# Transposed mixings of a four-layer graph network, done graph by graph on 64 rows of TensorE

## The reference

```python
h = relu(layernorm(x))
# layer 0: hypergraph convolutions: with H = (adj != 0), a node is mixed as D^-1 H B^-1 H^T (h @ W)
# layer 1: three graph convolutions
support = einsum('bnf,fh->bnh', h, W)
h = einsum('bnm,bmh->bnh', adj, support) + b
# layer 2: three diffusion steps with a learned transition matrix
# layer 3: mean of the neighbours, concatenated with x, times W
x = x + out
```

## Time and profile before

| | |
|---|---|
| median of 3 runs | 2702.6 us (2702.22 to 2703.21) |
| profiled execution, its own time | 2700.35 us |
| its span, first to last instruction | 2698.5 us |
| granted clock of TensorE | 0.999 of full |
| PE / PEld busy | 2655.7 us (98%) / 2218.4 us (82%) |
| DVE / ACT / POOL busy | 1924.8 (71%) / 1216.2 (45%) / 1153.9 us (43%) |

### The profile page before, as it was taken

One profiled execution on the slowest core, in us unless ns is written; L12 is line 12 of the kernel. 1 busy time (PEld: TensorE's weight loads), 2 busy tenths in 40 slices (PEclk: granted clock), 3 DMA queues, 4 the chain that ended last, 5 costly groups with the idle time before them and its releaser, 6 DMA issues.

```text
span 2698.5 us, 44877 instructions
## 1 busy us (share of the span) xinstructions
PE 2655.7 (98%) x13218; PEld 2218.4 (82%) x13218; DVE 1924.8 (71%) x4504; ACT 1216.2 (45%) x2231; POOL 1153.9 (43%) x2022
## 2 busy tenths in 40 slices
PE   7999999999999999999999998999999999999999
PEld 4888888888888888888888887888888888888887
DVE  7777777777777665656665668777777777777776
ACT  4444444434444554545454553322222222566665
POOL 5444444444444733333333346212112122677776
PEclk9999999999999999999999999999999999999999
DMA  4111111111111312111111122111111111344443
GB/s 136 39 40 47 38 38 36 45 45 35 41 33 44 109 34 66 37 62 43 56 45 54 49 82 88 57 54 54 56 52 48 54 54 64 114 148 152 134 139 124
DMA packets 136299, 178.58 MB, mean 66 GB/s; under 512 B 54464, under 2 KB 54464, under 8 KB 136256
## 3 DMA queue, kind: packets, MB, share of 16 engines
q1 hardware_dynamic: 131072, 168.62, 19.4%
q10 hardware_dynamic: 5184, 9.44, 1.2%
HBM read 110.90 MB, written 67.11 MB: 66 GB/s over the span
## 4 chain that ended last, share of the span: by engine, by line
PE 93%; DVE 2%; issue 1%; ACT 1%; POOL 1%; DMA 0%; SPq 0%; ACTq 0%; POOLq 0%; DVEq 0%
PE ps L464 27%; PE ps L466 27%; PE ps L465 26%; PE ps L481 6%; PE ps L506 4%; PE ps L484 2%; POOL w_lo L1272 1%; ACT row_hi L698 0%; DVE row_lo L948 0%; ACT w_hi L698 0%; PE ps L584 0%; PE ps L580 0%; ACT normed L738 0%; DVE adj_both L948 0%; POOL vecs L1297 0%
## 5 line engine op out<-in xcount | busy, mean ns | idle before, releaser
L464 PE MATMUL ps<-w_hi,col_hi 128*128 128x512 f32 x2752 | 1099.4, 399 | 2.6 <-POOL w_lo L1272 1.1
L466 PE MATMUL ps<-w_hi,col_lo 128*128 128x512 f32 x2752 | 1075.3, 391 | 0.0
L465 PE MATMUL ps<-w_lo,col_hi 128*128 128x512 f32 x2752 | 1072.5, 390 | 0.0
L466 PEld LDWEIGHTS ps<-w_hi,col_lo 128*128 128x128 f32 x2752 | 516.8, 188 | 112.5
L464 PEld LDWEIGHTS ps<-w_hi,col_hi 128*128 128x128 f32 x2752 | 517.4, 188 | 107.1 <-issue 5.1
L465 PEld LDWEIGHTS ps<-w_lo,col_hi 128*128 128x128 f32 x2752 | 518.4, 188 | 97.9 <-issue 0.2
L1305 POOL TENSOR_TENSOR var_eps<-moments,eps_ln 128x1 f32<-128x1 f32 x256 | 55.2, 216 | 924.4 <-DVE moments L965 924.4
L698 ACT ACTIVATE col_hi<-ps 128x512 fp32r<-128x512 f32 x448 | 255.5, 578 | 257.3 <-PE ps L484 133.8
L952 DVE TENSOR_TENSOR wide<-ps,col_hi 128x512 f32<-128x512 f32 x256 | 175.5, 686 | 146.9 <-ACT col_hi L698 145.5
L698 ACT ACTIVATE row_hi<-ps 128x512 fp32r<-128x512 f32 x224 | 132.9, 593 | 304.3 <-PE ps L466 302.9
L1272 POOL TENSOR_TENSOR row_lo<-normed,row_hi 128x512 fp32r<-128x512 f32 x128 | 165.1, 1301 | 214.0 <-ACT row_hi L698 213.9
(11 more groups left out here) (155 smaller groups left out, 4169.3 us busy)
## 6 DMA issues: line engine op xcount, KB each, us to landing
out<-x_res SPq DMA_DIRECT2D x256, 256.0 KB, 2.0
x_in<-out SPq DMA_DIRECT2D x192, 256.0 KB, 2.8
x_in<-x SPq DMA_DIRECT2D x64, 256.0 KB, 2.6
x_res<-out SPq DMA_DIRECT2D x64, 256.0 KB, 3.1
adj_in<-adj_t SPq DMA_DIRECT2D x96, 64.0 KB, 2.4
raw<-w ACTq DMA_DIRECT2D x12, 256.0 KB, 2.7
raw<-wk ACTq DMA_DIRECT2D x12, 256.0 KB, 2.7
raw<-w_t ACTq DMA_DIRECT2D x10, 256.0 KB, 3.0
```

The costliest lines, as they stand in the source:

```text
L464: nc.tensor.matmul(out_ap, lhs_hi, rhs_hi, start=start, stop=False, **checks)
L465: nc.tensor.matmul(out_ap, lhs_hi, rhs_lo, start=False, stop=False, **checks)
L466: return nc.tensor.matmul(out_ap, lhs_lo, rhs_hi, start=False, stop=stop, **checks)
```

## The change

The two graphs of a tile are mixed apart. For feature block `k` and graph `h`, the stationary operand is the 64 rows of that graph in `row_hi`, the moving one the graph's own 64x64 block of both halves of the adjacency (2x64 = 128 columns); with `row_lo` it is 64 columns. The result of graph 0 goes to bank 0 of the slot and that of graph 1 to bank 1. In the program, each such matmul stands in a tile of the array of 64 rows by 128 columns, at row 0 or at row 64; all others use 128 by 128. The readers of the result take the new layout (`graphs`, `halves`), and the semaphore counts twice, once for each graph.

```diff
         def halves(t):
-            both = ps[:, t, :, :].rearrange("p a (k h n) -> p (a k) h n", h=2, n=P)
-            return both[:, :, 0, :], both[:, :, 1, :]
+            both = ps[:, t, :, :].rearrange("p g (k h n) -> p g k h n", h=2, n=N)
+            return both[:, :, :, 0, :], both[:, :, :, 1, :]
+
+        def graphs(ap):
+            return ap.rearrange("p (k g n) -> p g k n", g=2, n=N)
...
-            def mix_transposed(t):
+            def mix_transposed(t, done):
                 for k in range(KB):
-                    at = ps[:, t, k // 2, (k % 2) * 2 * P:(k % 2 + 1) * 2 * P]
-
-                    nc.tensor.matmul(at, row_hi[:, t, k * P:(k + 1) * P],
-                                     adj_both[:, t, :, :].rearrange("p h n -> p (h n)"), start=k % 2 == 0, stop=False,
-                                     skip_group_check=True)
-                    last = nc.tensor.matmul(at[:, 0:P], row_lo[:, t, k * P:(k + 1) * P], adj_hi[:, t, :],
-                                            start=False, stop=True, skip_group_check=True)
-                return last
+                    of = slice(k * P, (k + 1) * P)
+                    for h in range(2):
+                        own = slice(h * N, (h + 1) * N)
+
+                        nc.tensor.matmul(ps[:, t, h, of], row_hi[own, t, of], adj_both[own, t, :, own],
+                                         start=k == 0, stop=False, skip_group_check=True)
+                    for h in range(2):
+                        own = slice(h * N, (h + 1) * N)
+                        last = nc.tensor.matmul(ps[:, t, h, k * P:k * P + N], row_lo[own, t, of], adj_hi[own, t, own],
+                                                start=False, stop=True, skip_group_check=True)
+                        if k == KB - 1:
+
+                            last.then_inc(done, 1)
...
-                    mix_transposed(t).then_inc(s1[name], 1)
+                    mix_transposed(t, s1[name])
...
-                    act.wait_ge(s1[name], i)
-                    copy(blocks(col_hi[:, t, :]), halves(t)[0]).then_inc(s1[name + "_hi"], 1)
+                    act.wait_ge(s1[name], 2 * i)
+                    copy(graphs(col_hi[:, t, :]), halves(t)[0]).then_inc(s1[name + "_hi"], 1)
...
-                V.tensor_tensor(blocks(left), halves(t)[0], blocks(f32(col_hi[:, t, :])), ALU.subtract).then_inc(left_done, 1)
+                V.tensor_tensor(graphs(left), halves(t)[0], graphs(f32(col_hi[:, t, :])), ALU.subtract).then_inc(left_done, 1)
                 dve.wait_ge(left_done, i)
-                return V.tensor_tensor(blocks(col_lo[:, t, :]), halves(t)[1], blocks(left), ALU.add)
+                return V.tensor_tensor(graphs(col_lo[:, t, :]), halves(t)[1], graphs(left), ALU.add)
```

More of the change, by code:

```diff
@@ L521, in hyper @@
                         pe.wait_ge(s["vec_out"], 2)
-                    mix_transposed(t).then_inc(s0["adj0"], 1)
+                    mix_transposed(t, s0["adj0"])
                 if name == "lin1":
@@ L748, in split @@
                 elif layer == 1:
-                    act.wait_ge(s1["adj2"], n(g, t) - SLOTS)
+                    act.wait_ge(s1["adj2"], 2 * (n(g, t) - SLOTS))
                 copy(row_hi[:, t, :], normed[:, t, :]).then_inc(s["split_hi"], 1)
@@ L764, in hyper @@
                 if name == "adj0":
-                    act.wait_ge(s0["adj0"], i)
-                    copy(blocks(col_hi[:, t, :]), halves(t)[0]).then_inc(s0["adj0_hi"], 1)
+                    act.wait_ge(s0["adj0"], 2 * i)
+                    copy(graphs(col_hi[:, t, :]), halves(t)[0]).then_inc(s0["adj0_hi"], 1)
                 if name in ("tra", "trb"):
@@ L792, in gcn @@
                     else:
-                        act.wait_ge(s1["adj2"], i - SLOTS)
+                        act.wait_ge(s1["adj2"], 2 * (i - SLOTS))
                     copy(adj_hi[:, t, :], adj_in[:, t, :]).then_inc(s1["asplit_hi"], 1)
                 if name in ("adj0", "adj1", "adj2"):
-                    act.wait_ge(s1[name], i)
-                    copy(blocks(col_hi[:, t, :]), halves(t)[0]).then_inc(s1[name + "_hi"], 1)
+                    act.wait_ge(s1[name], 2 * i)
+                    copy(graphs(col_hi[:, t, :]), halves(t)[0]).then_inc(s1[name + "_hi"], 1)
                 if name in ("bias0", "bias1"):
```

## The result

| | before | after |
|---|---|---|
| median | 2702.9 us (4 runs) | 2743.89 us (2743.33 to 2744.43, 4 runs) |
| span of the profiled execution | 2698.5 us | 2741.5 us |
| granted clock of TensorE | 0.999 | 0.997 |

What follows compares the result with a forecast made beforehand. TensorE was taken as the bound, its mixings paced by weight loads. 2700.4 + 236 (loads) + 0 (columns) + 0 (switching) = 2936 us, with the median 2.2 us above the profiled time: 2939 us, range 2690 to 2990.

Steps and rivals of the forecast that it cites:

- TensorE bounds, and a mixing goes by its loads: Transposed mixings: their TensorE cost reaches the end almost one to one, paced by weight loads at 0.115 us each.
- Columns cost and save nothing: Columns streamed in the mixings: they lie under the loads, so taken as nothing.
- Weight loads: Loads of a mixing call rise from 8 to 16: 236 us more taken, bounds from a 118 us gain.
- one step for each load: Mixing loads on 64 rows go in single file, 0.115 us each: 236 us more; chance 0.38 without further price.
- Switching: Changes to 64-row tiles and back, 352 in 176 runs of mixings: taken as nothing, at most 97 us.
- Rival 1: Mixings: the halves load together and the switch costs, 2710 to 2800 us, some 2750; chance 0.20.
- Other engines: ACT's copy and DVE's two passes after each mixing keep their 512 elements per partition; any added tens of ns hidden.
- The other side: Mixing loads on 64 rows are cheaper: 2692 us for a small gain, 2585 for full halving; chance 0.17.
- rival 4: Mixing loads on 64 rows cheaper; its small gain, 0.110 us a step with halves together, 10 us; family chance 0.17.

Runs made afterwards that it cites:

- wide_lo: Kernel before with row_lo multiplied by both halves of the adjacency (256 columns instead of 128), same eight weight loads a call: 2708.68 us, ratio 1.0027.
- all_rows: Changed kernel with its sixteen matmuls a mixing all on the full 128 rows of contraction, so no 64-row tiles and no switches: 2947.44 us, ratio 1.0917.
- modes_2: Changed kernel with feature blocks 0 and 2 of each mixing on 64-row tiles, 1 and 3 on full rows: 3061.72 us, ratio 1.1337.
- graph_after_graph: Changed kernel with the same sixteen 64-row matmuls, the eight of graph 0 first, then the eight of graph 1: 2874.9 us, ratio 1.0643.
- two_and_two: Changed kernel with, in each feature block, both matmuls of graph 0 and then both of graph 1: 2745.86 us, ratio 1.0165.

## Why the prediction was wrong

- *TensorE bounds, and a mixing goes by its loads:* right. What the mixings cost more reaches the end (40 of 41 us), DVE and ACT do not show, and wide_lo confirms the pace directly.
- *Columns cost and save nothing:* right within 7 us. The step read as even from the earlier trace rows does lean on the columns a little, from 0.119 us with the widest matmuls to 0.112 with the narrowest.
- *Weight loads:* this is the step that failed. I took "one step for each load", 236 us, because the loads of the earlier trace rows "form a single file"; but they all go into the same rows, and that they do so says nothing about loads into different ones. I had written that this was weak evidence, and still let it carry the forecast. One step for each load holds within the same rows (all_rows: 0.109 us for each added load); across halves the sixteen loads take the eight steps of before, so the term of 236 us is nothing, even 8 x 0.004 x 256 = 8 us the other way. What the Trainium skill says in "TensorEngine Tiling (Array Packing)", Key Properties, that tiles load in parallel, is borne out by the x2 rows, two loads in 0.19 us.
- *Switching:* taken at nothing with 97 us as bound. It is 0.31 us for a round trip between linear matmuls where 0.56 was the bound, for 146 of the 176 runs, and less for the other 30. The same page and section of the Trainium skill states a drain at a change of mode. The two gaps look like one; the rows show the gaps, not their cause. Rival 1, with 0.20, was the course of things and its 2710 to 2800 us held the result; the range from 2690 to 2990 held it also, but only because I had kept the other ends in it. The point was in the wrong case.
- *Other engines:* right, DVE's busy time is 1924.8 and 1924.6 us.
- *The other side:* the loads did come at 0.111 instead of 0.115, the small gain of rival 4; the switches ate it five times over. But it is hardly a gain of the 64 rows: under the same narrow matmuls loads on full rows come at 0.112 (all_rows), as the transposes of the earlier trace rows had them at 0.110. A mode that is entered for eight steps at a time pays only if its gain per run is above 0.31 us, and here it was 0.03 for a call: by an estimate from these two numbers, which no run tried, it would take runs of about ten calls.

## What to carry to other kernels

Before halving a matmul's columns, read whether columns or weight loads pace it: weight loads at nearly equal steps below matmuls of different width mean loads, and then only fewer loads, or loads that run together, help. Tiles of 64 rows hide a second load beside the first, which makes twice the loads free but not cheaper than half as many; and every entry and exit between linear matmuls costs 0.16 us on average, two thirds of a linear matmul of 512 columns, so they belong in long runs of work, not in single steps between full-array work. A price read from instructions that all share one resource isn't a price for instructions that don't.

## What the runs showed of the hardware that was not expected

**The clock falls while TensorE is busy all the time.** In all_rows (start and end us, width, PE, PEld, DVE, ACT, POOL busy us with instructions, granted clock, DMA):

```profile
1140.00:1155.00 15.00, 15.00 (x99) 13.54 (x99) 5.69 (x9) 6.54 (x12) 6.74 (x6) 1.00 0.29 97
1155.00:1159.00 4.00, 4.00 (x17) 3.32 (x17) 3.20 (x5) 1.12 (x2) 0.00 (x0) 0.60 0.19 62
1159.00:1174.00 15.00, 15.00 (x91) 13.27 (x90) 5.62 (x10) 5.32 (x10) 1.02 (x4) 0.99 0.00 0
```

TensorE was busy for all of the 15 us before the fall; but the fall, to the lower of its two levels (1.2 of 2.4 GHz, the 0.42 us between linear matmuls above), comes at the end of a run of mixings, in which small matmuls go at the pace of their loads. All 14 falls within layers 0 and 1 of this trace come in or right behind a run of two or three calls, and none at a run of one, although 112 of the 176 runs are of one. That such runs are what lowers it is suggested by this and by the kernels side by side, not shown by a kernel made for it. The kernels with more such steps have the lower mean clocks: 0.999 before, 0.984 with sixteen loads in file, 0.950 with two round trips a call. At the lower level the loads slow down too: one step is 0.213 us instead of 0.112 here. The page of modes_2 shows the falls by slices of its span, nine being 0.9 or more:

```profile
PEclk9999999999999999898889888899999999999999
```

The changed kernel itself lost next to nothing to it: 0.997 against 0.999 over the whole span, but full clock in the layers with the mixings.

**Loads pass each other.** Those for one half of the array overtake a few that are queued for the other half (three in graph_after_graph), so a program need not alternate strictly: two_and_two loses nothing.
